# Later tests, bank-by-bank products and earlier bank copies in a cross-attention and feed-forward kernel

## What is computed

```
h = gelu_tanh(x1) * x2          # x1, x2: both ln(x) @ ctx.T (120 wide)
x = x + h @ ctx                 # _layernorm(x) goes in
h = silu((n @ w1.T) * s1) * ((n @ w2.T) * s2)     # n = _layernorm(x); 256 -> 1024
h = gelu((h @ h1.T) * sh1)      # 1024 -> 1024, exact gelu
h = gelu((h @ h2.T) * sh2)      # 1024 -> 1024
x = x + (h @ w3.T) * s3         # 1024 -> 256
```

## Time and profile before

| | |
|---|---|
| median of 3 runs | 328.08 us (328.02 to 329.05) |
| profiled execution | 328.66 us |
| its span, first to last instruction | 326.9 us |
| TensorE busy (matmuls) | 316.8 us, 97% |
| VectorE busy | 265.1 us, 81% |
| ScalarE busy | 219.5 us, 67% |
| GpSimd busy | 59.6 us, 18% |
| chain that ended last, TensorE's share | 87% |
| moved by DMA | 74.91 MB, mean 229 GB/s |

### The profile page before, as it was taken

One profiled execution on the slowest core, in us unless ns is written; L12 is line 12 of the kernel. 1 busy time (PEld: TensorE's weight loads), 2 busy tenths in 40 slices (PEclk: granted clock), 3 DMA queues, 4 the chain that ended last, 5 costly groups with the idle time before them and its releaser, 6 DMA issues.

```text
span 326.9 us, 4932 instructions
## 1 busy us (share of the span) xinstructions
PE 316.8 (97%) x1628; PEld 225.9 (69%) x1628; DVE 265.1 (81%) x502; ACT 219.5 (67%) x369; POOL 59.6 (18%) x96
## 2 busy tenths in 40 slices
PE   7899999999999799999999999999999999999994
PEld 5699668756666366667998866886665666666893
DVE  4786996898981999997799675398799798998584
ACT  3567856565891794959934564977779688696840
POOL 5265013011211113213120003000211111120000
PEclk9999999999999999999999999999999999999999
DMA  6699999989999693999308054446999897994003
GB/s 211 248 231 244 207 257 365 416 273 371 333 357 406 223 307 82 276 353 281 105 15 309 3 184 146 185 128 231 274 264 294 306 341 237 215 218 132 0 28 110
DMA packets 31614, 74.91 MB, mean 229 GB/s; under 512 B 2144, under 2 KB 14176, under 8 KB 29024
## 3 DMA queue, kind: packets, MB, share of 16 engines
q0 software_dynamic: 21840, 52.43, 57.3%
q1 hardware_dynamic: 9744, 22.11, 19.7%
HBM read 71.39 MB, written 6.29 MB: 238 GB/s over the span
## 4 chain that ended last, share of the span: by engine, by line
PE 87%; DVE 5%; issue 2%; DMA 2%; ACT 2%; DVEq 0%
PE P L1407 27%; PE P L1389 25%; PE P L1342 18%; PE P L1446 5%; PE P L1433 4%; DMA SLY<-in_w 2%; PE P L1298 2%; PE P L1306 2%; PE P L1314 2%; DVE TL L967 1%; PE P L1455 1%; DVE H L960 1%; DVE H L1004 1%; ACT TH L648 1%; DVE SLY L1010 1%
## 5 line engine op out<-in xcount | busy, mean ns | idle before, releaser
L1407 PE MATMUL P<-TL,WR 128*128 128x512 f32 x448 | 111.9, 402 | 0.0
L1389 PE MATMUL P<-TH,WB 128*128 128x512 f16 x448 | 103.1, 380 | 2.5 <-ACT H L689 1.6
L1407 PEld LDWEIGHTS P<-TL,WR 128*128 128x128 f32 x448 | 84.1, 188 | 19.6
L648 ACT ACTIVATE TH<-H 128x512 f16<-128x512 f32 x112 | 67.8, 623 | 32.2 <-DVE H L960 29.7
L1389 PEld LDWEIGHTS P<-TH,WB 128*128 128x128 bf16 x448 | 41.1, 98 | 58.0 <-issue 7.7
L967 DVE TENSOR_TENSOR TL<-H,TH 128x512 fp32r<-128x512 f32 x112 | 73.7, 685 | 6.6 <-ACT TH L648 4.6
L1342 PE MATMUL P<-X,W 128*128 128x512 f32 (+1 forms) x320 | 62.5, 351 | 0.0
L1342 PEld LDWEIGHTS P<-X,W 128*128 128x128 f32 x320 | 51.8, 189 | 7.5
L960 DVE TENSOR_TENSOR H<-H 128x512 f32<-128x512 f32 x64 | 41.8, 682 | 0.0
L938 DVE SCALAR_TENSOR_TENSOR H<-P,sc,SLY 128x512 f32<-128x512 f32 (+1 forms) x40 | 25.3, 637 | 18.4 <-PE P L1342 10.5
L637 ACT ACTIVATE SLY<-P,sc 128x512 f32<-128x512 f32 (+1 forms) x40 | 24.1, 603 | 19.2 <-PE P L1342 15.9
(11 more groups left out here) (88 smaller groups left out, 257.9 us busy)
## 6 DMA issues: line engine op xcount, KB each, us to landing
WR<-blocks_h POOLq DMA_DIRECT2D x16, 1024.0 KB, 5.9
WR<-in_h POOLq DMA_DIRECT2D x11, 1024.0 KB, 7.3
WB<-blocks_h POOLq DMA_DIRECT2D x16, 512.0 KB, 4.9
WB<-in_h POOLq DMA_DIRECT2D x12, 512.0 KB, 7.5
H<-in_h POOLq DMA_DIRECT2D x8, 512.0 KB, 13.2
blocks_h<-H SPq DMA_DIRECT2D x4, 1024.0 KB, 6.5
SLY<-in_h SPq DMA_DIRECT2D x8, 512.0 KB, 4.9
SLY<-in_w SPq DMA_DIRECT2D x6, 512.0 KB, 7.3
```

What stands on the lines that cost most here:

```text
L648: eng.activation(TH[:, f % RING, :], operand(c, L, s, kk), ACT.Copy).then_inc(s_hi, 1)
L1389: out_ = eng.matmul(bank(c, L, s, m)[:, :], WB[r % WRING][:, at:at + 128], TH[:, f % RING, :], start=(s in FRESH[L] and kk == 0), stop=Fal ...
L1407: out_ = eng.matmul(bank(c, L, s, m)[:, :], WR[r % WRING][:, at:at + 128], TL[:, f % RING, :], start=False, stop=(kk == 3), skip_group_che ...
```

## The change

Three edits, none of which adds or removes an instruction of work. First, in `square`, the tests of steps 0 to 3 go behind the work of their step, on VectorE and on ScalarE. Second, the upper halves of products (0,5) and (0,6) run m outside and kk inside, so that they fill bank 0 with all four operand tiles, then bank 1, and so on; TH slots are released at the fourth bank. Third, in ScalarE's `late_products` the four `put_back` go ahead of the four `hi` of product (0,2), instead of alternating.

```diff
@@ -708,6 +708,7 @@
 
                 for i in range(4):
                     put_back(c, i)
+                for i in range(4):
                     hi(c, 0, 2, i)
                     if i == 2:
                         for n in beside(c, 0, 1):
@@ -737,13 +738,16 @@
 
                         if s == 0:
                             gelu(c, 0, (1, 0), i)
-                        if s < 6 and i == 0:
+                        if s in (4, 5) and i == 0:
                             for n in beside(c, 1, s):
                                 magnitude(n)
                         if 1 <= s <= 3:
                             snap(c, 1, s - 1, i)
                         if s < NP - 1:
                             hi(c, 1, s + 1, i)
+                        if s < 4 and i == 3:
+                            for n in beside(c, 1, s):
+                                magnitude(n)
                         if s == 4:
                             gelu(c, 1, (0, 1), i)
                         if s == 5:
@@ -1024,9 +1028,6 @@
             def square(c):
 
                 for s in range(NP):
-                    if s < 4:
-                        for n in beside(c, 1, s):
-                            test(n)
                     if (c, s) == (1, 0):
                         guard()
                     if c == 0 and s in (2, 3):
@@ -1038,6 +1039,9 @@
                             lo(c, 1, 3, i)
                         for i in range(4):
                             add(c, 1, 6, i)
+                    if s < 4:
+                        for n in beside(c, 1, s):
+                            test(n)
                     if c == 0 and s == 3:
                         scale(0, 4)
                     if s in (4, 5):
@@ -1378,17 +1382,30 @@
             def product(c, L, s):
                 r = entry(c, L, s)
                 upper_weights_in(eng, r)
-                for kk in range(4):
+
+                def upper(kk, m):
                     f = fill(c, L, s, kk)
-                    eng.wait_ge(s_hi, f + 1)
-
-                    for m in (2, 3, 0, 1) if (L, s, kk) == (0, 1, 0) else range(4):
-                        if kk == 0:
-                            bank_free(c, L, s, m)
-                        at = kk * 512 + m * 128
-                        out_ = eng.matmul(bank(c, L, s, m)[:, :], WB[r % WRING][:, at:at + 128], TH[:, f % RING, :],
-                                          start=(s in FRESH[L] and kk == 0), stop=False, skip_group_check=True)
-                    out_.then_inc(s_th, 1)
+                    if m == order[0]:
+                        eng.wait_ge(s_hi, f + 1)
+                    if kk == 0:
+                        bank_free(c, L, s, m)
+                    at = kk * 512 + m * 128
+                    out_ = eng.matmul(bank(c, L, s, m)[:, :], WB[r % WRING][:, at:at + 128], TH[:, f % RING, :],
+                                      start=(s in FRESH[L] and kk == 0), stop=False, skip_group_check=True)
+                    if m == order[3]:
+                        out_.then_inc(s_th, 1)
+
+
+                if (L, s) in ((0, 5), (0, 6)):
+                    order = (0, 1, 2, 3)
+                    for m in order:
+                        for kk in range(4):
+                            upper(kk, m)
+                else:
+                    for kk in range(4):
+                        order = (2, 3, 0, 1) if (L, s, kk) == (0, 1, 0) else (0, 1, 2, 3)
+                        for m in order:
+                            upper(kk, m)
 
                 if (L, s) == (0, 0):
                     weigh(4 * c + 2)
```

## The result

The changed kernel took 323.76 us (median of 4 runs, 323.47 to 324.10), against 328.05 us for the kernel before (median of 4, 327.59 to 329.05). The ratio is 0.9865, with a 95% interval of 0.984 to 0.9891: 4.3 us less. Forecast were 323.9, in a range of 323.1 to 325.4.

The account below looks back on a forecast made before the run. TensorE bounds the kernel nearly end to end, so only its waits can be recovered: 2.80 + 1.29 + 0.21 = 4.30, less 0.08, 4.2 us; 328.66 becomes 324.46, less 0.58 for the median: 323.9, range 323.1 to 325.4.

Parts of the forecast that it names:

- the six places: Places where TensorE's product starts stand further apart than clean: one loss of 2.80 us, five small of 0.20 to 0.58.
- The 2.80 us at (1,1): In c=0, product (1,1) waits behind a test's DMA; moving tests behind their product's work saves the whole 2.80 us.
- The 1.29 us of (0,5) and (0,6): Bank-by-bank upper halves want later banks later, so these stalls go: 0.40 + 0.31 + 0.58 = 1.29 us.
- The price of the order: Four matmuls in a row into one bank cost 0 to 0.16 us over 64 matmuls; 0.08 taken, 0.70 as an end.
- The 11 ns between the halves: Lower-half matmuls take 228 ns, rotating upper ones 217; by the skill's rule the difference belongs to the weight load.
- rival E: Same-bank matmuls wait for draining, 380 ns instead of 217: 7.8 us lost, net 3.5 slower, 331.6; chance 0.02.
- The 0.21 us of (0,2): ScalarE's copies into banks ahead of roundings fit its idle time; 0.21 us go in c=0, nothing in c=1.
- These are not independent: In c=0 small stalls before (1,1) would only have lengthened the wait there; they count because that wait is gone.
- The cover of 5.7 us at (1,2): Room at (1,2) for its first group, 113.1 - 107.4; a DMA landing more than 5.7 us later brings waits.
- Rival B: New wait at (1,2) if test 2's copy lands later; half of the 2.80 returned gives 325.3; chance 0.05.
- VectorE 2.3 us behind at (1,3): In c=0 VectorE's sums for (1,3) start at 133.20, TensorE ended that product at 130.89; could become 5.8 behind.
- rival D: VectorE is the bound behind and gives the 2.80 us back as waits: 326.7; chance 0.03.

Follow-up runs that it names:

- long holds: Load of test 2 issued only when product (1,0) of c=0 has ended: on the changed kernel 328.95 us, on the kernel before 338.23 us.
- banks_alone: The kernel before with only the bank-by-bank upper halves of (0,5) and (0,6): 327.10 us against 327.94, ratio 0.9972.
- copies_alone: The kernel before with only the four copies into banks ahead of the roundings of (0,2): 327.77 us against 327.94, ratio 0.999.
- tests_alone: The kernel before with only the tests of steps 0 to 3 moved, on VectorE and ScalarE: 325.30 us against 327.94, ratio 0.9914.
- after_all_magnitudes_last: The changed kernel with ScalarE's magnitudes of steps 4 and 5 of the second layer also behind their step's work: 331.05 us.

## Why the prediction was right, and where it was not

- *The number.* 323.9 against 323.76: closer than executions of one kernel agree (323.47 to 324.10), so the last 0.1 us is luck. The profiled executions differ by 4.8 us, not the 4.2 forecast: 0.54 of this is the earlier start and the shorter transposes, which the prediction did not have, and which the step down from the profiled execution to the median (0.58 before, 0.14 after) happened to take back. What bears the sum out is the starts: 4.29 us at the six places, 4.30 forecast.
- *The 2.80 us at (1,1).* Right in mechanism and size: 14.24 us for the two products with the tests moved, alone or with the rest. The long holds show the cause itself: a later magnitude costs the kernel before its full delay, 7.25 us for 7.26. That both queues had to be cleared was half right. At (1,1) VectorE's alone gave 2.67 of the 2.80, with a transfer that was 0.6 us quicker; ScalarE's is needed for the last stage, and for some 0.7 us at (1,1) when the transfer takes its 7.09 (the estimate above).
- *The 1.29 us of (0,5) and (0,6).* Right, each upper half is clean in the changed kernel and in banks_alone. But the reading of when the fourth bank of (0,5) is wanted was off: 40.94 is the start in the chain, and the timeline has 40.78. From there it is wanted at 41.43, and the copy that ends at 41.58 costs 0.20 us; by the 41.59 of the prediction it would have cost next to nothing.
- *The price of the order, 0.08, at most 0.16 by the nearest rows.* Nothing that the start times can show (3.28 against 3.27 us for 16). The 11 ns between the halves do not belong to the bank; that they belong to the load of f32 weights would fit the rule of the Trainium skill that the text weighed (TensorE: Matmul & The Clock Gate, Weight-path perf modes), but no run here separated it from the halves' other difference, the moving operand (f32 instead of 16-bit). The rule on rotating banks (the Trainium skill, Perfetto Trace Analysis, Optimizing Tensor Performance, Matmuls) speaks of independent groups; read against four in a row of one group, as in rival E, it is not borne out by 3.28 us for 16.
- *The 0.21 us of (0,2).* Right, and below what a median can tell.
- *"These are not independent", all small waits of c=0 swallowed by the one at (1,1).* Wrong as put. Only what (0,6) gains is swallowed; the load of test 2 is issued 4.46 to 4.47 us behind the start of (0,6) in every kernel without a hold, so what is gained earlier moves it too (the starts in banks_alone and copies_alone show it, not their times). It changed nothing in the sum.
- *The cover of 5.7 us at (1,2).* It is 4.3, and it was the wrong place to look for the nearest danger: the last stage of c=0 has 2.4 us, and the serial chain of loads (each needs the test two before it) carries a delay there. Rival B looked for the new wait at (1,2); it comes there too once the load is late enough, but the last stage has less room.
- *VectorE 2.3 us behind at (1,3)*. In the changed kernel these sums start at 127.26 while (1,3) ends at 127.04, so VectorE caught up instead of falling behind, as the text against rival D said.
- *The lower end of the range.* 328.08 less 4.30 is 323.8, and 0.3% below that is 322.8, not 323.1. The measured time lies inside either.

## What to carry to other kernels

Work that nobody waits for, but that waits for a DMA, belongs behind the work of its step on every in-order queue it stands in; and check what else is chained to its end, since here the next load but one hangs on it. Behind is not a rule: in steps 4 and 5 the test stands ahead of useful work on VectorE, and there a later magnitude cost 7.3 us. For a group of matmuls over several banks, go bank by bank where the banks come free late and the operands are early, and operand by operand where it is the other way round; the order itself was free.

## What the runs showed of the hardware

A 512 KB load took 7.1 to 7.2 us from its issue to its use when issued at 96 us, and 4.8, 4.3 and 3.9 us when issued at 99, 100 and 106: holding it back by 3.3 us made its user start only 0.5 us later. Between kernels that issue it at the same point it varied from 6.2 us (tests_alone, 96.21 to 102.42) to 7.2.

After an idle stretch of 7.69 us TensorE came back at a granted clock of 0.50 and ran 13 matmuls in 5.64 us instead of 2.98; in the 6 us with waits of 0.86 and 1.47 us in the last stage (after_all_magnitudes_last) the clock shows 0.72. The waits of 0.5 to 0.7 us at (1,1) of the kernel before left the mean clock of its profiled execution at 0.999.

A bank that comes free late costs what the timeline's start says, not the chain's, which stands some 0.15 us later: (0,5) of c=0 lost 0.20 us to a copy that ended 0.15 after 40.78 + 0.65.

Four matmuls in a row into one bank (bf16 weights, 512 columns) took 3.28 us for 16, going round four banks 3.27.
